# Expert stage of a two-layer transformer kernel: order of weighing, routing, zeroing and share turns, and one value product ahead of an output product

## The reference, cut to what matters

```python
probs = softmax(tok @ gate_w.T)
topv, topi = top_k(probs, 2)
topw = topv / (sum(topv) + 1e-09)
combine = zeros((T, E)).at[arange(T)[:, None], topi].set(topw)
eg, eu = einsum('td,eid->eti', tok, wg), einsum('td,eid->eti', tok, wu)
eo = einsum('eti,edi->etd', silu(eg) * eu, wd)
moe_out = einsum('te,etd->td', combine, eo)
```

## Time and profile before

| | |
|---|---|
| median of 3 runs | 623.61 us (623.31 to 623.74) |
| the profiled execution's own time | 623.53 us |
| its span, first to last instruction | 621.6 us |
| granted TensorE clock, mean | 0.986 |
| busy share: PE, PE weight loads, DVE, ACT, POOL | 95%, 80%, 61%, 56%, 34% |
| share of the chain that ended last: PE, DVE, ACT | 84%, 5%, 5% |

### The profile page before, as it was taken

How to read it: one execution, slowest core, us unless ns; L and a number is a source line. 1 busy time by engine, 2 the same in 40 slices (tenths; PEclk the granted TensorE clock), 3 DMA queues, 4 the chain that set the end, 5 groups by cost and what they waited for, 6 DMA issues and landing times.

```text
span 621.6 us, 13499 instructions
## 1 busy us (share of the span) xinstructions
PE 590.2 (95%) x5498; PEld 498.3 (80%) x5498; DVE 376.8 (61%) x676; ACT 346.7 (56%) x876; POOL 213.5 (34%) x226
## 2 busy tenths in 40 slices
PE   4789999999999989999998999999999998999996
PEld 3678888888888878888877888888788887788885
DVE  4577778777877566786845253262515276683475
ACT  0678668866885554543546453555445455555552
POOL 0672544254426523453434040131303026432200
PEclk9799999999999899999999999999999999999999
DMA  7760000000000139445101030102120001210023
GB/s 206 274 253 29 1 3 2 3 1 3 1 2 2 28 114 289 127 137 174 51 0 44 27 102 2 34 26 78 41 64 1 2 0 36 68 35 0 1 84 122
DMA packets 13677, 38.36 MB, mean 62 GB/s; under 512 B 2320, under 2 KB 3856, under 8 KB 13008
## 3 DMA queue, kind: packets, MB, share of 16 engines
q1 hardware_dynamic: 13376, 36.46, 17.9%
q10 hardware_dynamic: 240, 1.05, 0.7%
HBM read 36.39 MB, written 1.11 MB: 60 GB/s over the span
## 4 chain that ended last, share of the span: by engine, by line
PE 84%; DVE 5%; ACT 5%; DMA 2%; issue 2%; SPq 0%; ACTq 0%; POOL 0%; DVEq 0%
PE ps L1597 20%; PE ps L1599 19%; PE ps L1598 19%; PE ps L1715 9%; PE ps L1915 4%; PE ps L1674 3%; PE ps L1692 2%; PE ps L1704 2%; PE ps L1903 1%; DVE strm_lo L1415 1%; DMA work<-in_cols 1%; ACT strm_hi L965 1%; PE ps L1626 1%; PE ps L1753 1%; ACT w_hi L684 1%
## 5 line engine op out<-in xcount | busy, mean ns | idle before, releaser
L534 POOL TENSOR_TENSOR w_lo<-raw_w,w_hi 128x1024 fp32r<-128x1024 f32 x24 | 58.6, 2459 | 159.8 <-ACT w_hi L684 139.3
L1415 DVE SCALAR_TENSOR_TENSOR strm_lo<-ps,col,strm_hi 128x512 fp32r<-128x512 f32 x32 | 24.0, 750 | 104.4 <-ACT strm_hi L965 103.4
L1597 PE MATMUL ps<-w_hi,act_hi 128*128 128x512 f32 (+1 forms) x192 | 74.1, 386 | 5.3 <-ACT junk L677 3.1
L1599 PE MATMUL ps<-w_hi,act_lo 128*128 128x512 f32 (+1 forms) x192 | 71.5, 372 | 0.0
L1598 PE MATMUL ps<-w_lo,act_hi 128*128 128x512 f32 (+1 forms) x192 | 71.4, 372 | 0.0
L950 ACT ACTIVATE work<-ps,col 128x512 f32<-128x512 f32 x64 | 43.9, 688 | 44.6 <-PE ps L1599 44.6
L1597 PE MATMUL ps<-act_hi,w_hi 128*128 128x512 f32 x160 | 63.5, 397 | 3.4 <-ACT work L950 2.0
L1715 PE MATMUL ps<-raw_w,xT 128*128 128x256 f32 x256 | 62.9, 387 | 0.0
L1598 PE MATMUL ps<-act_lo,w_hi 128*128 128x512 f32 x160 | 62.4, 390 | 0.0
L1599 PE MATMUL ps<-act_hi,w_lo 128*128 128x512 f32 x160 | 62.4, 390 | 0.0
L1715 PEld LDWEIGHTS ps<-raw_w,xT 128*128 128x128 f32 x256 | 47.5, 194 | 5.9
(11 more groups left out here) (204 smaller groups left out, 1428.1 us busy)
## 6 DMA issues: line engine op xcount, KB each, us to landing
raw_w<-in_w_attn SPq DMA_DIRECT2D x20, 512.0 KB, 4.0
raw_s<-in_w_moe SPq DMA_DIRECT2D x11, 384.0 KB, 5.2
work<-comb_dram SPq DMA_DIRECT2D x21, 128.0 KB, 2.9
raw_w<-in_w_qkv SPq DMA_DIRECT2D x4, 512.0 KB, 6.5
raw_w<-in_w_o SPq DMA_DIRECT2D x1, 2048.0 KB, 8.7
work<-comb_dram SPq DMA_DIRECT2D x8, 256.0 KB, 4.9
raw_s<-in_w_ffn SPq DMA_DIRECT2D x8, 256.0 KB, 2.8
bd<-in_w_ada SPq DMA_DIRECT2D x1, 1536.0 KB, 6.5
```

What stands on the lines that cost most here:

```text
L534: G.tensor_tensor(flat(w_lo[:, slot]), raw, flat(f32(w_hi[:, slot])), ALU.subtract).then_inc(s_piece_lo, 1)
L1415: V.scalar_tensor_tensor(flat(strm_lo[:, n % SS]), ps[:, 4 + n % 2, :], c_("bv", 4 * UNITS[u][0] + h), flat(f32(strm_hi[:, n % SS])), ALU. ...
L1597: mm(dst, ah, bh, start=start and i == 0, stop=False, **flags)
L1599: last = mm(dst, al, bh, start=False, stop=stop and i == len(terms) - 1, **flags)
```

## The change

Five edits, all of order:

1. VectorE: `route0` is split. At n = 1 the order becomes hu(1), weigh_hi(0), the shift of tile 7's logits, weigh_hi(1), weigh_lo(0), the shares of tile 7 (all the small operations), weigh_lo(1), and then hu(2).
2. ScalarE: hidden_hi(0) moves from behind gate(2) to between route_exp and gate(2).
3. GpSimd: the zeros of `bd` move from ahead of the unit loop to turn 8 of it, behind a wait for moe_up(7).
4. TensorE: turn_comb(1) moves from ahead of down(0) to between down(0) and down(1).
5. TensorE, last attention unit only: pv1(6, 2) moves ahead of out1(6, 0).

```diff
+        ZERO_TURN = 8
...
-            pool.wait_ge(s_ada_mm, 1)
-            G.memset(bd[:], 0.0).then_inc(s_bd_zero, 1)
             for n in range(NM):
+                if n == ZERO_TURN:
+                    pool.wait_ge(s_moe_u, n)
+                    pool.wait_ge(s_ada_mm, 1)
+                    G.memset(bd[:], 0.0).then_inc(s_bd_zero, 1)
                 for f in range(SS, MI):
...
             route_exp(slice(EARLY, TILES), 2)
+            hidden_hi(0)
             gate(2)
...
-                if n != NM - 2:
+                if n not in (1, NM - 2):
                     hidden_hi(n - 1)
...
-            def route0(g, count):
+            def route0_shift(g):
                 dve.wait_ge(s_glog, g.stop)
                 src = ps[:, 3, g.start * NE:g.stop * NE].rearrange("p (t e) -> p t e", e=NE)
                 shifted(src, None, g).then_inc(s_gsh, 1)
+
+            def route0_shares(g, count):
                 dve.wait_ge(s_gexp, count)
                 probs_value(g)
                 probs_index(g)
...
                 if n == 1:
-                    route0(slice(EARLY, TILES), 2)
-                    weigh(0)
-                if n < 1:
+                    weigh_hi(0)
+                    route0_shift(slice(EARLY, TILES))
+                    weigh_hi(1)
+                    weigh_lo(0)
+                    route0_shares(slice(EARLY, TILES), 2)
+                    weigh_lo(1)
+                if n <= 1:
                     continue
...
                 if n == 3:
+                    moe_down(0)
                     turn_comb(1)
-                    moe_down(0)
...
                 if u >= 1:
+                    if u == U - 1:
+                        pv1(u - 1, 2)
                     out1(u - 1, 0)
-                    pv1(u - 1, 2)
+                    if u < U - 1:
+                        pv1(u - 1, 2)
                     out1(u - 1, 1)
```

More of the change, by code:

```diff
@@ L1293, in route0 @@
                 V.tensor_tensor(rt[:, 9, g], rt[:, 7, g], rt[:, 8, g], ALU.add).then_inc(s_comb, 1)
-            route0(slice(0, EARLY), 1)
+            route0_shift(slice(0, EARLY))
+            route0_shares(slice(0, EARLY), 1)
             add_h(EARLY)
@@ L1315, in weigh_lo @@
                                 ALU.subtract).then_inc(s_hm_ready, 1)
-            def weigh(n):
-                weigh_hi(n)
-                weigh_lo(n)
             def residual1(a):
```

## The result

The changed kernel took 620.99 us (median of 22 executions) against 623.91 for the kernel before, taken beside it: 2.92 us less, a ratio of 0.9946 with a 95% interval from 0.9929 to 0.9964. The forecast was 620.5, with 3.02 us less. Each kernel had one execution far out, 1355.17 us after the change and 1173.07 before, which the ratio leaves out. The interval alone would allow a gain of 2.2 to 4.4 us, so that the two numbers agree to 0.1 us is in part luck. What bears on the forecast are the distances within one trace.

The account below looks back on a forecast made before the run. TensorE, busy nearly throughout, was taken as the bound, so only its idle places could gain: 2.19 us in the expert stage plus 0.83 in the last attention unit, 3.02 off 623.53, giving 620.5, range 619.9 to 621.9.

Parts of the forecast that it names:

- Free to up(4): Expert stage, from TensorE free behind up(3) until up(4) starts: 5.40 us before, forecast to shrink by 2.19 us.
- the margins: Four spare times of 0.35 to 0.85 us in the expert stage, among them weigh_lo(1) 0.5 and the shares 0.85.
- the rival of the thin margin: Expert stage: slow CAST or late weigh_hi(3) uses up the spare time, costing 0.7 or 1.0 us; 620.9 to 622.0, chance 0.18.
- Unit 3, feared to be late next: Expert stage: later share turning puts weigh_hi(3) at risk; unit 3 forecast ready at 235.05, wanted at 235.40, 0.35 us spare.
- what edit 3 is worth: VectorE's routing of tile 7: moving GpSimd's zeros away was to shorten the 1.40 us CAST by 1.2 us.
- The zeros' new place: GpSimd, turn 8: zeros at about 247.3 to 250.8, priced at nothing; rival that they hold VectorE's multiplications: 0.7 us, chance 0.04.
- Edit 5: 0.83 forecast: Last attention unit on TensorE: pv1(6, 2) fits into idle time ahead of out1(6, 0), so out1(6, 3) starts 0.83 us earlier.
- VectorE's chain behind head 3's remainder: Last attention unit: softmax1_tail(7), which releases pv1(7, 0), was to move along by 0.83 us; otherwise the gain is near 0.
- The wait ahead of out1(6, 0): Last attention unit: TensorE's 1.42 us idle before this product was to fall to some 0.6 us.
- Slower: Expert stage rival: routing stands behind weigh_hi(0) and weigh_hi(1), which wait for loads of shares; 624 to 626 us, chance 0.03.
- The larger case: Late loads of shares in the expert stage: from 3.9 us late the whole gain is gone; a landing of 8.9 gives 625.7.

Follow-up runs that it names:

- e3: The changed kernel with the zeros back ahead of GpSimd's unit loop; TensorE free to up(4) 3.30 us, profiled 623.85 us.
- e2: The kernel before with only pv1(6, 2) moved ahead of out1(6, 0); 623.02 against 624.49 us, ratio 0.9983.
- e9: The kernel before with only the new VectorE order and hidden_hi(0) moved on ScalarE; TensorE free to up(4) 3.82 us, profiled 621.89 us.
- e8: The changed kernel run again, unaltered, on the chip of the early-value-product run; 622.98 us, ratio 0.9953 to the kernel before.
- e1: The changed kernel without the attention edit, so the four expert-stage edits alone; 623.37 against 624.49 us, ratio 0.9974.
- e4: The changed kernel with turn_comb(1) ahead of down(0) again; TensorE free to up(4) 3.73 us, profiled 619.33 us.
- e6: The changed kernel with hidden_hi(0) behind gate(2) again on ScalarE; TensorE free to up(4) 4.41 us, profiled 623.77 us.
- e5: The kernel before with only the zeros moved to turn 8; TensorE free to up(4) 4.23 us, profiled 623.52 us.
- e7: The changed kernel with head 3's value product ahead of head 1's output product in every attention unit; 616.66 against 625.48 us, ratio 0.9867.
- e10: The changed kernel with head 3's value product early in every attention unit and the zeros in their old place; 619.01 against 623.70 us, 0.9905.

## Why the prediction was right, point by point

**Free to up(4): 2.19 forecast, 2.10 measured.** Measured from the moment TensorE is free, in us:

| | forecast | after |
|---|---|---|
| shares of tile 7 ready | 0.59 | 0.33 |
| weigh_lo(1) over | 1.24 | 0.92 |
| turn starts | 1.43 | 1.44 |
| down(1) starts | 1.78 | 1.79 |
| copy of the turned shares starts | 2.09 | 2.07 |
| up(4) starts | 3.21 | 3.30 |
| weigh_hi(3) starts | 7.70 | 7.70 |

The queue of each engine was followed rightly, and the three rows that hold the gain are within 0.1 us. The only term off is down(1), 1.51 against 1.43, taken from another unit; down(1) stands right behind the turn, and its first matmul occupies 0.20 (225.23 to 225.43) instead of 0.12. The routing and weigh_lo(1) were quicker than added up, by 0.3, so the margins were wider than feared, and the rival of the thin margin fell. Unit 3, feared to be late next, was ready 0.44 us before TensorE wanted it (233.22 against 233.66); 0.35 was forecast.

**A step that was wrong without moving the sum: what edit 3 is worth.** The forecast took 1.2 us off the shares because the zeros, which hold the CAST, move away. It never asked where the CAST would lie with the zeros in their old place. e3 leaves them there, the CAST takes 0.17, and the front is still 3.30. The sum came out right because the 1.2 was counted once, whichever edit saves it: its owner was wrong, and in this the forecast was lucky. The forecast's own rows could have told: the CAST starts 1.08 behind the first operation of the shares (220.82 to 221.90), and the forecast let the shares start at 222.8. That puts the CAST at 223.9, behind the zeros' end at 223.28 even in their old place.

**The zeros' new place: nothing, as priced.** They came at 246.53, not 247.3 less the common shift, because the low part in front of them waited for ScalarE until 245.64, only 0.25 us earlier relative to TensorE's free time, where the forecast had it 1.4 earlier. That cost nothing. The two weigh_hi inside them took 0.69 us each, and 0.68 and 0.69 in e3. That speaks against what the Trainium skill says in "GPSIMD Engine Reference", section "Key points", where GpSimd contends with VectorE instructions of two SBUF inputs, and agrees with what the Trainium skill says in "SBUF — State Buffer", section "SBUF: two separate sides", which limits the case to GpSimd operations that read SBUF. But the move has a by-product: the low part pushed behind the zeros ran beside weigh_lo(8) and stretched it to 1.84 us, where e3, with the zeros in front, has 0.92; the earlier trace rows show the same kind of stretch. TensorE did not wait for it. Edit 3 is thus neutral in the new order, as far as the scatter of 0.3 us lets one tell: middle 298.16 with it and 298.13 without.

**Edit 5: 0.83 forecast, 0.93 measured.** out1(6, 3) starts 5.43 behind out1(6, 0), not 6.36: 0.93 earlier. The 0.10 more is in the output products: out1(6, 0) and out1(6, 1) in a row occupy 2.81 (517.97 to 520.78), where the forecast had twice 1.46. VectorE's chain behind head 3's remainder moved with it, as assumed: the wait ahead of pv1(7, 0) is 0.22, as before. The wait ahead of out1(6, 0) was to be some 0.6: 1.42 - 0.83. It is shown as 0.34 in e2, where pv1(6, 2) and the gap take 1.49 (518.79 to 520.28), 0.66 more than 0.83. In the changed kernel it appears as 0.48 within pv1(6, 2). out1(6, 0) follows the modulation by 0.21 us (517.25 + 0.51 to 517.97), and by 0.15 before: at most 0.06 lost.

**Slower, because weighing now stands ahead of the routing:** the loads of shares were not late in the changed kernel. weigh_hi(0) and weigh_hi(1) ran without a wait shown. e9 shows this rival in small, 0.12 us late on VectorE. The larger case was not seen in any trace.

## What to carry to other kernels

When two long waits of the bounding engine end on one busy helper engine, look at what that helper does in between: here a chain of small operations that nobody needed yet stood ahead of two operations that the bounding engine was waiting for. Follow the whole cross-engine chain: without the one ScalarE copy moved beside it, half of the gain was gone. If two edits remove the same conflict, undo each alone before keeping both, and when the gain is smaller than the scatter of the runs, measure it between two rows of one trace.

## What the runs showed of the hardware

**The stages ahead of the change scatter with the clock.** TensorE was free behind up(3) at any time from 223.30 to 228.62 us, in kernels that hardly differ ahead of that point; the changed kernel and e8, which are the same, have 223.44 and 227.42. Rows of the windows view (stretch, length, busy us of PE, PE weight load, DVE, ACT, POOL, then granted clock, DMA share, GB/s), the changed kernel's first, then e8's:

```profile
0.00:60.00 60.00, 46.31 (x646) 38.45 (x647) 42.34 (x73) 35.23 (x124) 25.93 (x27) 0.89 0.57 197
...
200.00:223.00 23.00, 22.25 (x145) 18.93 (x139) 14.22 (x62) 14.63 (x29) 10.12 (x14) 1.00 0.26 88
```

```profile
0.00:60.00 60.00, 47.98 (x632) 39.80 (x633) 35.02 (x68) 31.86 (x111) 25.93 (x27) 0.80 0.57 197
...
200.00:223.00 23.00, 22.36 (x147) 19.19 (x147) 13.99 (x51) 12.95 (x29) 12.54 (x16) 0.93 0.17 46
```

The clock granted in the first 60 us orders the twelve profiles for the most part: 0.91 in e1, e2 and e4 (free at 223.3 to 223.7), 0.89 in after, before and e6 (223.4 to 225.9), 0.86 in e9 (225.2), 0.83 in e5, e7 and e10 (226.3 to 228.6), 0.80 in e3 and e8 (227.4 and 228.3). From 60 to 200 us all have 1.00. Before, e3, e6, e8 and e10 have a second dip ahead of the free time, 0.93 over 200 to 223, and the others 1.00. At 0.89, before and e6 with this dip are free at 225.3 and 225.9, and the changed kernel without it at 223.4. e10, the last of all at 0.83, is out of order even so. The dip is a few us at the lower of the engine's two levels, 1.2 GHz, ahead of the first share turn. In the trace of before:

```profile
206.00:207.00 1.00, 1.00 (x4) 0.81 (x3) 0.96 (x7) 1.00 (x3) 1.00 (x2) 0.50 0.00 0
```

TensorE shows a wait of 0.7 to 0.8 us for that turn in the seven profiles without the dip, and none in the five with it. That is the new entry in the list of waits of the changed kernel.

Clock and time go together in runs without a trace too: of the changed kernel's executions, five at a mean clock of 0.977 or 0.978 took 623.6 to 624.5 us, and three at 0.989 to 0.991 took 618.2 to 619.7. So the two kernels overlap run by run, though their medians are 2.9 us apart, and e7 could beat e8 by 6.3 us of median time with 3.8 us less in its middle and 0.7 less behind it. What makes the clock come out one way or the other was not tried.

**A wait costs more than it shows.** 0.19 shown was a gap of 0.34 in each attention unit, and the output product behind it took 0.14 longer than in e7's order. The 1.56 us of the two waits in the earlier trace rows went with 2.1 us of the front.

**Zeros held a CAST, but no multiplication.** Beside the same fill a CAST of 8 columns waited until its end (1.40 and 1.41 in the two profiles with the old order and place, 0.17 in the ten others), and multiplications of 128 x 512 with both inputs in SBUF ran at full speed (0.68 and 0.69).

**A value product was split.** Right behind the scores' small matmuls, pv1(6, 2) ran as five passes, 0.48 us of nothing that the profile explains, and three passes, and so in e10; in e3 the pause was 0.31. In e2, e4 and e8 it ran in one piece, of 1.16, 1.29 and 1.43 us, where such a product takes 1.05 elsewhere. The cause stays open. The cost was at most 0.06 us, since the modulation was the later release.
